# A mixture-of-experts kernel on one core: the first token tile's turn between two halves, the first unit's rows in other buffers, idle matmuls on TensorE

## What is computed

```python
# 1: attention with a sigmoid, on 8 batches of 256 x 512
s = jax.nn.sigmoid(einsum('bdn,bdm->bnm', layernorm(x), ctx) / sqrt(256))
x = x + tanh(g_xattn[0]) * einsum('bvn,bnm->bvm', ctx, s)
# 2: experts, on M = 2048 tokens of 512
xf = layernorm(x)
t = xf * rsqrt(mean(xf * xf) + EPS) * norm_w
vals, idx = top_k(t @ gate_w.T + gate_b, 4)
G = zeros.at[tokens, idx].set(softmax(vals))
h = einsum('mh,eoh->emo', t, w1) + b1          # 1024 values per expert and token
a, b = minimum(h[..., ::2], 7), clip(h[..., 1::2], -7, 7)
y = einsum('emi,edi->emd', a * sigmoid(1.702 * a) * (b + 1), w2) + b2
x = x + tanh(g_ffn[0]) * (xf + einsum('me,emd->md', G, y))
```

## Time and profile before

| what | value |
|---|---|
| median of 3 runs | 843.23 us (842.14 to 843.66) |
| the profiled execution | 844.3 us |
| its span, first to last instruction | 842.5 us |
| mean granted clock of TensorE | 0.959 |
| busy in the span: TensorE, VectorE, ScalarE, GpSimd | 91%, 62%, 55%, 38% |

### The profile page before, as it was taken

One profiled execution on the slowest core, in us unless ns is written; L12 is line 12 of the kernel. 1 busy time (PEld: TensorE's weight loads), 2 busy tenths in 40 slices (PEclk: granted clock), 3 DMA queues, 4 the chain that ended last, 5 costly groups with the idle time before them and its releaser, 6 DMA issues.

```text
span 842.5 us, 16653 instructions
## 1 busy us (share of the span) xinstructions
PE 766.3 (91%) x4028; PEld 654.3 (78%) x4029; DVE 520.2 (62%) x1020; ACT 459.7 (55%) x785; POOL 317.8 (38%) x290
## 2 busy tenths in 40 slices
PE   5999997059999999999999999999999999999984
PEld 2666575048888899988888888898998988898873
DVE  3898885425676575566576665756556575746540
ACT  3565654025566564556557655646556565656540
POOL 0266775631324315242324333334333333325212
PEclk9998998568999999999999999999999999999997
DMA  7656663042577576347649645556535555544223
GB/s 283 196 193 201 210 177 114 10 131 78 128 210 172 111 215 162 62 129 207 137 149 230 174 104 130 147 137 154 145 67 146 107 150 134 155 124 75 37 25 38
DMA packets 107767, 117.00 MB, mean 139 GB/s; under 512 B 11808, under 2 KB 77344, under 8 KB 107744
## 3 DMA queue, kind: packets, MB, share of 16 engines
q1 hardware_dynamic: 88896, 77.32, 29.7%
q0 software_dynamic: 18848, 39.40, 23.8%
HBM read 88.06 MB, written 28.94 MB: 139 GB/s over the span
## 4 chain that ended last, share of the span: by engine, by line
PE 76%; DVE 7%; POOL 6%; issue 5%; ACT 3%; DMA 1%; another core or an unknown queue 0%; DVEq 0%; POOLq 0%; ACTq 0%
PE ps L543 41%; PE ps L492 25%; POOL tab L1138 5%; PE ps L471 4%; PE ps L407 3%; PE ps L395 2%; PE ps L390 1%; DVE uu L1062 1%; DVE hv L1064 1%; DVE W1l L1073 1%; ACT bw L711 1%; DVE bv L1060 1%; ACT hTh L731 1%; DMA xg<-rows,srcI 0%; PE ps L424 0%
## 5 line engine op out<-in xcount | busy, mean ns | idle before, releaser
L543 PE MATMUL ps<-xTh,W1h 128*128 x768 | 257.9, 336 | 13.8 <-issue 11.5
L543 PE MATMUL ps<-xTl,W1h 128*128 x768 | 252.2, 328 | 0.0
L543 PE MATMUL ps<-xTh,W1l 128*128 x768 | 252.0, 328 | 0.0
L1220 POOL DMA_INDIRECT out<-ys,dgI x75 | 118.9, 1585 | 309.9 <-ACT ys L690 287.0
L543 PEld LDWEIGHTS ps<-xTh,W1h 128*128 128x128 f32 x768 | 146.0, 190 | 24.7 <-issue 19.6
L543 PEld LDWEIGHTS ps<-xTl,W1h 128*128 128x128 f32 x768 | 146.1, 190 | 5.3
L543 PEld LDWEIGHTS ps<-xTh,W1l 128*128 128x128 f32 x768 | 145.8, 190 | 5.5
L492 PE MATMUL ps<-W2h,hTh 128*128 x300 | 119.8, 399 | 7.7 <-DVE hTl L1068 7.7
L690 ACT ACTIVATE ys<-ps,dgI 128x512 f32<-128x512 f32 x75 | 51.6, 689 | 121.9 <-DVE ps L1033 115.8
L492 PE MATMUL ps<-W2l,hTh 128*128 x300 | 117.6, 392 | 0.0
L492 PE MATMUL ps<-W2h,hTl 128*128 x300 | 117.5, 392 | 0.0
(11 more groups left out here) (140 smaller groups left out, 1066.5 us busy)
## 6 DMA issues: line engine op xcount, KB each, us to landing
W1f<-in_wts SPq DMA_DIRECT2D x64, 512.0 KB
W2f<-in_wts SPq DMA_DIRECT2D x32, 512.0 KB
X<-in_x SPq DMA_DIRECT2D x8, 512.0 KB
Kt<-in_ctx SPq DMA_DIRECT2D x8, 512.0 KB
Vt<-in_ctxT SPq DMA_DIRECT2D x8, 512.0 KB
rows<-tt SPq DMA_DIRECT2D x8, 512.0 KB
out<-base SPq DMA_DIRECT2D x8, 512.0 KB
b2s<-in_bias SPq DMA_DIRECT2D x16, 256.0 KB
```

The lines of the kernel that those rows point to most:

```text
L543: m = e.matmul(P_[i % 2][:, 0:32 * w], (W1h, W1l)[wl][:, i, 2 * k + h, :], (xTh, xTl)[xl][:, bass.ds(par, 1), k, 0:32 * w], start=(t == 0) ...
L1220: e.indirect_dma_start(out, bass.IndirectOffsetOnAxis(dgI[:, j, 0:1].bitcast(I32), axis=0), ys[j][:], None, compute_op=ALU.add).then_inc(d ...
```

## The change

- TensorE runs 17 matmuls whose result nobody reads before the first product; the memsets that make their operands go first on VectorE.
- The first unit's rows are gathered into ys[0..3] with row numbers in src0 and semaphores d_first; GpSimd's wait for the four turns before the second unit's gathers goes away. A wait for a_base is added before the first gathers.
- TensorE waits for the landing of idx, runs 5 idle matmuls of 256 columns, and after each of the first four turns 1 more, after the last 3.
- The wait for xTl stands inside the branch of the first pair; turned_in(0) stands between its PA and PB halves, in each of the six widths. ScalarE does high_x of that tile between av and bw, VectorE low_x before hidden(0).

```diff
--- before.py
+++ after.py
@@ -130,6 +130,7 @@
         Ri = sb("Ri", [128, E], I32)
         b1s = sb("b1s", [128, E, 3, 4])
         bcur = sb("bcur", [128, 3, 4])
+        src0 = sb("src0", [128, 4, 2])
         srcI = sb("srcI", [128, 4, 2])
         dgI = sb("dgI", [128, 4, 2])
         idx = sb("idx", [128, (E + 1) * TE + 3, 2])
@@ -221,6 +222,7 @@
         d_b, d_b1 = sem("d_b"), sem("d_b1")
         d_idx0, d_idx, d_s = sem("d_idx0"), sem("d_idx"), sem("d_s")
         d_g = [sem(f"d_g{j}") for j in range(4)]
+        d_first = [sem(f"d_first{j}") for j in range(4)]
         e_src, e_dg = sem("e_src"), sem("e_dg")
 
         v_mh, v_zero, v_ones, v_su, v_mm0 = sem("v_mh"), sem("v_zero"), sem("v_ones"), sem("v_su"), sem("v_mm0")
@@ -435,6 +437,13 @@
                 e.matmul(RK[:, 32:64], SUb[:], mk[:, b, :, :].rearrange("p j e -> p (j e)"), start=True, stop=False)
                 e.matmul(RK[:, 32:64], many[:], MM[:, b, :, :].rearrange("p j e -> p (j e)"), start=False, stop=True).then_inc(t_rank, 1)
 
+            def run_idle(n):
+                for _ in range(n):
+                    e.matmul(ps[0][:, 0:256], idm, C[:, 0:256], start=True, stop=True)
+
+            e.wait_ge(v_ones, 1)
+            for _ in range(17):
+                e.matmul(RK[:], ones[:], many[:].unsqueeze(1).broadcast_to((128, 4, 128)), start=True, stop=True)
             for b in range(B):
                 for c in range(3):
                     qk(b, c)
@@ -465,10 +474,10 @@
             e.matmul(at(F_NT), ones[0:E, :], Q2[:].rearrange("p r t -> p (r t)"), start=False, stop=False)
             e.matmul(LG[:, 64 + F_NT * NUP:64 + F_NT * NUP + NUP], ones[0:E, :], Q3[:], start=False, stop=True).then_inc(t_te, 1)
 
-            def turn_x(j, r, P_=PX):
+            def turn_x(j, r, from_=xg, P_=PX):
                 e.wait_ge(e_xl, r)
                 for c in range(4):
-                    m = e.transpose(P_[:, 128 * c:128 * c + 128], xg[j][:, 128 * c:128 * c + 128], idm)
+                    m = e.transpose(P_[:, 128 * c:128 * c + 128], from_[j][:, 128 * c:128 * c + 128], idm)
                 m.then_inc(e_tx, 1)
 
             def second_layer(hidden):
@@ -500,7 +509,7 @@
             landed = many_regs(e, "pe_landed", 4)
             turned, done = e.alloc_register("pe_turned"), e.alloc_register("pe_done")
             for r in landed:
-                e.reg_mov(r, 16)
+                e.reg_mov(r, 0)
             e.reg_mov(turned, 4)
             e.reg_mov(done, 0)
             load_fields(e, now, 0, 0)
@@ -508,9 +517,12 @@
             e.reg_mov(was[F_NT], 0)
             e.reg_mov(was[F_X], 0)
             e.reg_mov(was[F_S2], 0)
+            e.wait_ge(d_idx0, 16)
+            run_idle(5)
             for j in range(4):
-                e.wait_ge(d_g[j], 16)
-                turn_x(j, 1, P0[j])
+                e.wait_ge(d_first[j], 16)
+                turn_x(j, 1, ys, P0[j])
+                run_idle(1 if j < 3 else 3)
             e.wait_ge(e_lop, 3)
             with e.Fori(0, n) as u:
                 par = e.snap(u % 2)
@@ -521,21 +533,21 @@
                     with e.If(more > LESS[j]):
                         e.reg_add(turned, turned, 1)
                         e.reg_add(landed[j], landed[j], 16)
-                        come, free = e.snap(landed[j], min_val=32, max_val=16 * NTILES), e.snap(turned, min_val=5, max_val=NTILES + 24)
+                        come, free = e.snap(landed[j], min_val=16, max_val=16 * NTILES), e.snap(turned, min_val=5, max_val=NTILES + 24)
                         e.wait_ge(d_g[j], come)
                         turn_x(j, free)
 
                 ready = e.snap(e.snap(turned, min_val=4, max_val=NTILES + 24) + 1)
                 for i in range(4):
                     made, read = e.snap(x_ * N1 + (i + 1)), e.snap(u * 4 + (i + 1))
-                    if i == 0:
-                        e.wait_ge(e_xl, ready)
                     e.wait_ge(e_lo1, made)
                     e.wait_ge(e_af, read)
                     e.wait_ge(e_bf, read)
                     e.sem_inc(e_gp, 1)
 
                     def part(w):
+                        if i == 0:
+                            e.wait_ge(e_xl, ready)
                         for h, P_, q in ((0, PA, e_l1a), (1, PB, e_l1b)):
                             t = 0
                             for k in range(4):
@@ -544,6 +556,8 @@
                                                  (xTh, xTl)[xl][:, bass.ds(par, 1), k, 0:32 * w], start=(t == 0), stop=(t == 11))
                                     t += 1
                             m.then_inc(q, 1)
+                            if i == 0 and h == 0:
+                                turned_in(0)
 
                     def pick(ws):
                         if len(ws) == 1:
@@ -557,7 +571,6 @@
 
                     pick(WIDTHS)
                     if i == 0:
-                        turned_in(0)
                         second_layer(e.snap(u * 4 + 4))
                     if i < 3:
                         turned_in(i + 1)
@@ -702,11 +715,13 @@
                 last = e.snap(now[F_LAST], min_val=0, max_val=1)
                 fresh = e.snap(was[F_LAST], min_val=0, max_val=1)
 
-                def gate(i, w):
+                def gate(i, w, between=None):
                     now_ = e.snap(u * 4 + (i + 1))
                     e.wait_ge(e_l1a, now_)
                     e.activation(sg[i % 2][:, 0:w], PA[i % 2][:, 0:w], AF.Sigmoid, scale=ALPHA, bias=bcur[:, 2, i:i + 1]).then_inc(e_sg, 1)
                     e.activation(av_[i % 2][:, 0:w], PA[i % 2][:, 0:w], AF.Identity, bias=bcur[:, 0, i:i + 1]).then_inc(e_af, 1)
+                    if between:
+                        between()
                     e.wait_ge(e_l1b, now_)
                     e.activation(bw[i % 2][:, 0:w], PB[i % 2][:, 0:w], AF.Identity, bias=bcur[:, 1, i:i + 1]).then_inc(e_bf, 1)
 
@@ -747,8 +762,7 @@
                 e.copy(bcur[:], b1s[:, bass.ds(x_, 1), :, :].rearrange("p o h c -> p (o h) c")).then_inc(e_bc, 1)
                 e.wait_ge(e_bc, e.snap(u + 1))
                 e.sem_inc(e_ga, 1)
-                by_width(lambda w: gate(0, w))
-                turned_in(0)
+                by_width(lambda w: gate(0, w, lambda: turned_in(0)))
                 second()
                 turned_in(1)
                 next_high(0)
@@ -897,10 +911,10 @@
                     e.wait_ge(e_hi2, c - N1 + 1)
                     e.tensor_tensor(W2l[:, 0, half2(c)], W2f[:, 0, half2(c)], W2h[:, 0, half2(c)].bitcast(F32), ALU.subtract).then_inc(e_lo2, 1)
 
+            e.memset(ones[:], 1.0)
+            e.memset(many[:], float(TE)).then_inc(v_ones, 1)
             for q in hv:
                 e.memset(q[:], 0.0).then_inc(v_zero, 1)
-            e.memset(ones[:], 1.0)
-            e.memset(many[:], float(TE)).then_inc(v_ones, 1)
             e.memset(MM[:, 0, 0, :], 0.0).then_inc(v_mm0, 1)
             ln_stats(0, 0)
             ln_stats(0, 1)
@@ -1156,7 +1170,7 @@
             put(B - 1)
 
             def place(col, r):
-                e.tensor_copy(srcI[:], idx[:, col:col + 4, :] if isinstance(col, int) else idx[:, bass.ds(col, 4), :]).then_inc(e_src, 1)
+                e.tensor_copy(srcI[:], idx[:, bass.ds(col, 4), :]).then_inc(e_src, 1)
                 e.wait_ge(e_src, r)
                 e.sem_inc(e_go, 1)
 
@@ -1167,9 +1181,11 @@
             for i in range(2):
                 e.wait_ge(d_rows[i], 16 * (B // 2))
             e.wait_ge(d_zrow, 16)
-            place(0, 1)
+            e.wait_ge(a_base, 2 * B)
+            e.tensor_copy(src0[:], idx[:, 0:4, :]).then_inc(e_src, 1)
+            e.wait_ge(e_src, 1)
             for j in range(4):
-                gather(j)
+                e.indirect_dma_start(ys[j][:], None, rows, bass.IndirectOffsetOnAxis(src0[:, j, 0:1].bitcast(I32), axis=0)).then_inc(d_first[j], 16)
             e.wait_ge(v_te, 3)
             e.wait_ge(d_idx, 16)
             n = units(e)
@@ -1196,7 +1212,6 @@
                         e.reg_add(given, given, 1)
                         gather(j)
 
-            e.wait_ge(e_tx, 4)
             place(row(nxt), 2)
             gathers(nxt)
             e.wait_ge(d_zero, 16)
```

## The result

The changed kernel takes 835.13 us (median of 4 runs, 833.78 to 835.44), the kernel before in the same job 842.73 us (842.14 to 843.66). The ratio is 0.9903, 95% interval 0.9887 to 0.9919: 7.6 us faster by the medians, inside the range, 3.3 us above the forecast. The profiled execution took 835.31 us, its span is 833.5 us (before 844.3 and 842.5), and the mean granted clock is 0.969 (0.959).

The account below looks back on a forecast made before the run. Time was seen in the start and the road into the loop, on TensorE and its clock. Gains 2.3 + 10.1 - 1.0 = 11.4 us off the profiled 844.3 gave 832.9, 831.8 us as median; range 827.4 to 837.8.

Parts of the forecast that it names:

- Start: Kernel's start: after 17 idle matmuls the first group's 16 instructions run 0.43 us apart; gain 2.3 us, bounds 0 and 2.3.
- the start gives nothing: Rival at the start: VectorE's chain, a late load or the idle matmuls eat the gain; 834.1 us, chance 0.15.
- Road: From idx landing to the first unit's turn 2: idle matmuls, later xTl wait and earlier turn 0 gain 10.1 us.
- number 3: Entry to the first pair: wait for e_xl behind other waits and branches costs 0.4 us instead of 1.47; bounds 0.05 and 1.47.
- step 6: First unit: pair 1 starts at 184.05 instead of 191.48 us, at the high clock, and ends at 189.0; gain 10.1 us.
- The rival with 0.25: First unit's turns: clock stays at 1.2 GHz through them, road gains 7.0 instead of 10.1 us; 834.9 us, chance 0.25.
- The loop: Units' loop: turn 0 in mid-pair exposes 0.17 us of issue in a quarter of units; cost 1.0 us, bounds 0 and 23.5.
- The slower rival: Loop: TensorE's queue stalls in the middle of pair 0, 0.8 us per unit, 18.4 us in all; 849.2 us, chance 0.04.

Follow-up runs that it names:

- e9: Kernel before plus only the start's 17 idle matmuls, loop code placed by a never-taken branch; 841.08 us, ratio 0.9982.
- e8: Changed kernel plus 8 idle matmuls before the last second layer and ScalarE's d_base wait behind its register loads; 831.58 us, ratio 0.9855.
- e10: Kernel before with only turn 0 between pair 0's halves and the later xTl wait, loop placed by a never-taken branch; 840.24 us, ratio 0.9970.
- e11: Changed kernel without the idle matmuls around the first unit's turns, loop placed by a never-taken branch; 837.05 us, ratio 0.9932.
- e12: Changed kernel with turned_in(0) and the xTl wait back in their old places, loop placed by a never-taken branch; 838.13 us, ratio 0.9944.
- e6: Kernel before with only turn 0 between pair 0's halves and the later xTl wait, plus 78 executed semaphore increments; 840.68 us, ratio 0.9966.
- e7: Changed kernel without the idle matmuls around the first unit's turns, plus 44 executed semaphore increments; 837.62 us, ratio 0.9932.

## Why the prediction was right, and where it was off

**Start: right.** 2.3 us were forecast; line 397 begins at 22.80 us, where line 395 stood at 25.05: 2.25 us. The 17 matmuls took 6.76 us (6.8 forecast) and ended before Qt, and the 16 instructions took 7.13 us (7.05). That the first of these agrees is partly luck: the row read for it holds 24 matmuls and no turn (the turn is the one that ends it, at 199.12), 0.32 us each, and "under 0.4" was a rounding up; the 17 took 0.40 each. It reaches the copy of idx in part: in the nine traces with the start's part that copy stands at 165.2 us on average, in the five without at 166.8, 1.6 us apart, and the median of e9 says 1.5. But single traces scatter over 2.9 us in the first group and 2.3 in the second. The rival "the start gives nothing" is out by line 397 and by e9, whose interval ends at 0.9995.

**Road: the mechanism right, 1.9 us of 10.1 missing.** In the forecast turn 2 came 21.5 us after idx, in the trace 23.4. By steps:
- idx to the first matmul: 10.8 forecast, 11.3 measured. The turns were done sooner than I said and xTl ended 10.0 us after idx, not 10.4. The step that failed is number 3, the wait behind the branches, priced at 0.4 us: the first matmul came 1.26 us after xTl. What was late is TensorE's own branch on the width. Line 567, all its compare-and-branches (duration min, median, max in ns):

```profile
L567 PEldq COMPARE_BRANCH  x332: 64/173/2026, 173.9 to 801.8; - x166
```

The one of 2026 ns runs from 174.2 to 176.3 us, at the first entry into the loop, and a packet of the instruction queue lies at 173 to 174 us. The same branch at the loop's entry takes 1321 ns in e8, 2984 in e10 and 3364 in e11; before, where the wait for xTl stood ahead of it, none there is over 373 ns.

How much the moved wait was worth can be read from the time between the end of xTl and the first matmul:

| wait for xTl | kernel: us from xTl to the first matmul |
|---|---|
| ahead of the branches | before 1.47, e9 1.34, e12 1.35 |
| behind them | after 1.26, e8 0.78, e10 1.99, e11 2.36, e6 0.21, e7 0.22 |

In the changed kernel it gave 0.1 us against e12, where 1.07 were forecast, and in e10 and e11 it was a loss. In e6 and e7, whose turns came late, the entry's branch took 3.0 and 2.9 us too, but it had ended (by 180.7 and 176.4 us) before xTl was done (180.96 and 176.91), and there the first matmul follows at once. So the wait and the branches do run beside each other, as meant; but in the changed kernel this branch begins only at 174.2 us, when the last turn has ended (174.0), and it outlasts xTl (175.4).

That code loading is what takes the 2 us is argued from the packet and from it being the first pass; no run took it away. The Trainium skill (Advanced Engine Details and Errata, Control Flow Timing) gives about 108 ns for a compare-and-branch; the median here is 173 ns.
- The first matmul to turn 1: 5.4 forecast, 5.56 measured, with no wait for xTl and none for the gather, which went at 173.46 (175.7 forecast; counted from the copy of idx, 8.1 us against 8.2).
- Turn 1 to pair 1: 0.35 forecast, 1.50 measured, with 0.87 us idle for issue. This is step 6's start at 184.05, and the larger half of the miss. The trace of before showed it: 0.70 us of issue at the same place, at 191.48. I took pair 1 from the turn's price alone and read that row only for its time. e8, e10, e11 have 1.14, 1.01 and 0.83 there.
- Pair 1 to turn 2: 4.95 forecast, 5.05 measured.

**The clock.** The rival with 0.25, that it stays low through the turns, did not happen: the granted clock is 0.96 in the mean from 170.6 to 175.3 us, and 1.00 from 176.7. The after trace alone can't say whether turns or idle matmuls held it there, since the idle ones went first; e6 shows that transposes alone can raise it. They don't always: in e11, 4.2 us of turns from 170.1 us left it at 0.50, up to 182.7, and in e7, 3.65 us of turns from 171.9 left it there up to 181. What sets the two pairs of runs apart was not found. So the idle matmuls before the turns do what they are for, and e11 gives their worth, 2.4 us by the medians and 3.4 by the trace.

**The loop: nearly free.** 1.0 us was charged; the trace has 0.4 between turn 2 and the last second layer. Issue waits went from 8.0 to 8.5 us, and one wait for a gather of 0.48 us is new, at 449.67: turn 0 asks for its rows half a pair sooner. The slower rival, a stalled queue in the middle of pair 0, would have cost 0.8 us in each of 23 units.

**What the forecast left out: the tail, 0.9 us.** The cold stretch behind the last wait for hTl was 3.4 us long before and 6.8 after. The prediction read the 3.6 us wait at the end and not the clock behind it. e8 shows what it is worth: 2.8 us with idle matmuls in it.

**Sum.** Against the profiled executions, 11.4 us forecast and 9.0 found: start -0.2, road -1.9, loop +0.6, tail -0.9, together -2.4. The other 0.9 us up to the 3.3 between the medians is that the profiled execution after lies 0.2 us over its median, and not 1.1 as before.

## What to carry to other kernels

Where an engine waits for its own bank behind another engine's long work, moving the producer up by half a step removes the wait and the cold clock that the wait leaves behind; price the two together: here 2.95 us for the stand and 2.3 to 2.6 for the cold pair (7.64 us before and 7.30 in e12, 5.05 after). Idle matmuls were tried here only in stands that the timeline shows, sized to end about when the work behind them is ready: the start, the road and the tail gave 2.3, 3.4 and 2.8 us in the traces. A branch into code that runs for the first time is priced by itself, from the same place in the trace, and not as one more branch. And before a part is judged by leaving it out, look at the instruction queue: if its packets have gone from a dozen to hundreds, the run measures where the code lies and not the part.

## What was not expected of the hardware

- **Where the loop's code lies can cost 36%.** Four variants of kernels that take 835 and 843 us took 1148 to 1152; three of them, with unused instructions in a branch never taken ahead of the loop, are back at 837 to 841. Some 8 packets of 16 KB come anew in each unit, and TensorE stands 212 us for issue ahead of one group instead of 11.5. Why these places reload and those don't was not settled.
- **A semaphore increment on TensorE is not free in number:** 0.15 us each, from stands of 20.45, 9.41 and 6.82 us with 111, 39 and 22 of them; 218 of them in a branch that is not taken cost nothing that could be measured (idx to turn 2: 31.4 us in e9, 31.6 before).
- **The first pass into code has its own price:** one branch of 1.3 to 3.4 us at the loop's entry in six traces (after, e6, e7, e8, e10, e11), against a median of 0.17 us. In the three that have the wait for xTl ahead of the branches (before, e9, e12) none at the entry is over 0.37 us, and the longest, 1.6 to 2.5 us, comes elsewhere.
- **Clock drops in the attention part move:** one of 6.7 us at 71.1 us before, at 85.7 us after, two in others (70.1 and 104.2 us in e11). TensorE worked nearly through them (6.70 of 6.70 us before, 6.49 of 6.70 after). Each comes near a wait of TensorE for tTs: 1.14 us up to 70.0 before, 2.42 up to 85.9 after, 1.13 up to 67.9 and 0.93 up to 102.7 in e11; but e11 has one of 1.11 us up to 86.0 with no drop behind it. What sets them off stays open; they may be the cause of the 2.9 us by which the landing of idx scatters, which was not tested.
